# Summing three products of weights and values: one VectorE operation over a strided view in place of two additions

## The reference

```python
def attn(x, ...):                          # H = 16 heads, DH = 16
    xp = x @ Wp.T + bp
    q = ((xp @ Wq.T + bq) * scale).reshape(b, s, H, DH)
    k, v = ...                             # in the same way
    idx = stack([(i - 1) % s, i, (i + 1) % s], axis=1)
    kn, vn = k[:, idx], v[:, idx]
    attn = softmax(einsum('bshd,bsnhd->bshn', q, kn), axis=-1)
    out = einsum('bshn,bsnhd->bshd', attn, vn).reshape(b, s, d)
    return out @ Wo.T + bo

x = x + 0.5 * ffn(layernorm(x))
x = x + attn(layernorm(x))
x = x + 0.5 * ffn(layernorm(x))
```

## Time and profile before

| | us |
|---|---|
| median of 3 runs | 1087.7 (1087.16 to 1088.61) |
| the profiled execution's own time | 1087.54 |
| its span, first to last instruction | 1085.7 |
| TensorE busy | 1033.5 (95%) |
| VectorE busy | 861.3 (79%) |
| GpSimd busy | 716.6 (66%) |
| ScalarE busy | 544.9 (50%) |

### The profile page before, as it was taken

The page is one execution under the profiler, slowest core; times in us unless marked ns, Lnnn a source line. Parts: engine busy times, 40 slices in busy tenths (PEclk is TensorE's granted clock), DMA queues, the critical chain, the costliest instruction groups (busy, mean ns, idle before and its releaser), DMA issues.

```text
span 1085.7 us, 17486 instructions
## 1 busy us (share of the span) xinstructions
PE 1033.5 (95%) x5277; PEld 850.7 (78%) x5277; DVE 861.3 (79%) x2405; ACT 544.9 (50%) x1219; POOL 716.6 (66%) x956
## 2 busy tenths in 40 slices
PE   5889899999999999999999999999999999999785
PEld 3677788888888888888888888888888888887663
DVE  3648888888888888888888888888888888888882
ACT  4264455554545555554555555445555554544431
POOL 3366677666668777666777666677777766664453
PEclk9899999999999999999999999999999999999998
DMA  5001000000000000000000000000000000000000
GB/s 169 11 28 37 15 21 20 3 19 21 21 20 21 20 15 7 20 20 21 20 21 20 13 9 20 20 21 20 20 21 1 21 20 20 11 11 10 11 10 20
DMA packets 12613, 23.02 MB, mean 21 GB/s; under 512 B 2244, under 2 KB 5844, under 8 KB 12520
## 3 DMA queue, kind: packets, MB, share of 16 engines
q1 hardware_dynamic: 9240, 13.37, 3.5%
q0 software_dynamic: 3280, 8.53, 2.8%
HBM read 12.46 MB, written 8.39 MB: 19 GB/s over the span
## 4 chain that ended last, share of the span: by engine, by line
PE 87%; DVE 6%; issue 2%; DMA 1%; ACT 1%; SPq 0%; POOL 0%; DVEq 0%; POOLq 0%; ACTq 0%
PE ffn_bank L906 20%; PE ffn_bank L908 20%; PE ffn_bank L907 20%; PE tr_bank L935 5%; PE mix_bank L906 4%; PE mix_bank L908 4%; PE mix_bank L907 4%; PE tr_bank L948 3%; PE mix_bank L980 2%; PE tr_bank L906 1%; PE tr_bank L907 1%; PE tr_bank L908 1%; DMA we_raw<-in_L_ffn_We 1%; PE tr_bank L955 1%; DVE chain_sum L674 1%
## 5 line engine op out<-in xcount | busy, mean ns | idle before, releaser
L906 PE MATMUL ffn_bank<-we_hi,T_hi 128*128 128x512 f32 x1024 | 410.4, 401 | 3.8 <-DVE chain_sum L674 3.0
L908 PE MATMUL ffn_bank<-we_hi,T_lo 128*128 128x512 f32 x1024 | 401.3, 392 | 0.0
L907 PE MATMUL ffn_bank<-we_lo,T_hi 128*128 128x512 f32 x1024 | 400.8, 391 | 0.0
L465 ACT ACTIVATE we_raw<-ffn_bank,gate 128x256 f32<-128x256 f32 x512 | 207.4, 474 | 159.2 <-PE ffn_bank L908 159.0
L346 POOL TENSOR_TENSOR chain_sum<-chain_sum,we_raw 128x512 f32<-128x512 f32 x128 | 166.2, 1299 | 125.0 <-DVE chain_sum L674 124.7
L906 PEld LDWEIGHTS ffn_bank<-we_hi,T_hi 128*128 128x128 f32 x1024 | 193.0, 189 | 44.0 <-DVE chain_sum L674 4.6
L908 PEld LDWEIGHTS ffn_bank<-we_hi,T_lo 128*128 128x128 f32 x1024 | 193.0, 188 | 41.9
L907 PEld LDWEIGHTS ffn_bank<-we_lo,T_hi 128*128 128x128 f32 x1024 | 193.4, 189 | 35.2
L674 DVE SCALAR_TENSOR_TENSOR chain_sum<-ffn_bank,gate,chain_sum 128x256 f32<-128x256 f32 x256 | 111.4, 477 | 36.4 <-PE ffn_bank L908 36.4
L323 POOL TENSOR_TENSOR var_eps<-mean_var,eps 128x2 f32<-128x2 f32 x96 | 29.1, 303 | 151.3 <-DVE mean_var L594 151.3
L423 ACT CAST T_hi<-tr_bank 128x512 fp32r<-128x512 f32 x128 | 72.1, 590 | 106.6 <-PE tr_bank L935 86.3
(11 more groups left out here) (129 smaller groups left out, 1716.3 us busy)
## 6 DMA issues: line engine op xcount, KB each, us to landing
out_x<-y SPq DMA_DIRECT2D x31, 256.0 KB
we_raw<-in_L_ffn_We SPq DMA_DIRECT2D x2, 1024.0 KB, 13.9
x_in<-in_L_attn_x,x_row POOLq DMA_INDIRECT x60
x_in<-in_L_attn_x SPq DMA_DIRECT2D x2, 256.0 KB, 6.5
moved_qk<-qk SPq DMA_DIRECT2D x4, 124.0 KB
w_raw<-in_L_attn_Wq SPq DMA_DIRECT2D x1, 256.0 KB, 3.0
w_raw<-in_L_attn_Wk SPq DMA_DIRECT2D x1, 256.0 KB, 3.3
w_raw<-in_L_attn_Wv SPq DMA_DIRECT2D x1, 256.0 KB, 4.0
```

What stands on the lines that cost most here:

```text
L465: last = nc.scalar.activation(scaled[:, f, t, half, j], ffn_bank[b][:, j * D:(j + 1) * D], ACT.Copy, scale=gate[:, 2 * f + t, e:e + 1])
L906: nc.tensor.matmul(dest, hi[:, t, k, :], w_hi_[:, k, c0:c1], start=(first and k == 0), stop=False, skip_group_check=not first)
L907: nc.tensor.matmul(dest, hi[:, t, k, :], w_lo_[:, k, c0:c1], start=False, stop=False, skip_group_check=not first)
L908: last = nc.tensor.matmul(dest, lo[:, t, k, :], w_hi_[:, k, c0:c1], start=False, stop=(k == KB - 1), skip_group_check=not first)
```

## The change

The two additions become one `tensor_reduce` that adds along the innermost dimension of a rearranged view of `prod`: for each of the 512 output numbers the three inputs are 512 numbers (2 KiB) apart. It waits for count 14, where the first addition waited for 13, and raises the count by 2, so that a group still has 16 counts. The wait for `T_done[TO]` stands before it.

```diff
             def value_sum_step(a):
                 ops = attn_ops
-                dve.wait_ge(ops, a.times(ATTN_OPS, 13))
-                nc.vector.tensor_tensor(prod[:, 0], prod[:, 0], prod[:, 1], ALU.add).then_inc(ops, 1)
-                dve.wait_ge(ops, a.times(ATTN_OPS, 15))
+                dve.wait_ge(ops, a.times(ATTN_OPS, 14))
                 await_(dve, T_done[TO], a.times(1))
-                nc.vector.tensor_tensor(attn[:], prod[:, 0], prod[:, 2], ALU.add).then_inc(ops, 1)
+                nc.vector.tensor_reduce(attn[:].rearrange("p t n -> p (t n)"), prod[:].rearrange("p m t n -> p (t n) m"),
+                                        AX.X, ALU.add).then_inc(ops, 2)
```

## The result

The changed kernel takes 1090.9 us in the median of nine runs (1089.62 to 1092.96), against 1088.61 us for nine runs of the kernel before on the same footing (1086.52 to 1089.28). The ratio is 1.0026, with a 95% interval of 1.0017 to 1.0034: some 2.8 us slower, between 1.8 and 3.7 (the two medians are 2.3 us apart, the two means 3.0). The forecast was +1.6 us, to 1089.3 us, and "within 0.2%" as the likeliest; the time lies on the forecast side and in the range, a little beyond the 0.2%. Of the 1.6 us between 1089.3 and 1090.9, 0.9 are the base: the forecast stood on 1087.7 us, the median of three runs, and the nine runs of the kernel before have 1088.61.

A forecast was written before the change was run, and what follows sets the result against it. TensorE was taken to bound 130 to 967 us, so savings there count nothing; in the drain VectorE's sum lies on the path, 3 x 0.52 = +1.6 us on 1087.7, making 1089.3 us, range 1087.3 to 1093.5.

The forecast's parts named there:

- within 0.2%: Whole kernel: time differs from the kernel before by no more than about 0.2% (2.2 us); given 0.58.
- TensorE bounds the steady part: 29 groups outside the drain, fill included: some 15 us of saved VectorE time goes into idle time, gain nothing.
- The three groups of the drain carry the loss: Groups 29, 30 and 31: each ends its sum 0.52 us later, all passed on to TensorE, +1.6 us.
- The wait for the third product: Drain steps: waiting for count 14 rather than 13 makes the reduction begin 0.13 us later than line 747 did.
- The reduction's length: The new VectorE reduction of 1536 elements: taken as 1.80 us, ends 1.74 and 3.2 us.
- The first rival: Three drain steps: hops cost a turn each, reduction up to 3.2 us, +5.8 us, kernel 1093.5 us; chance 0.20.
- The second rival: Drain, behind TensorE's longer waits: granted clock falls once more, 1.7 us, kernel 1091.0 us; chance 0.15.

The follow-up runs named there:

- e1: Kernel before with the reduction in the 29 groups outside the drain, the two additions kept in groups 29, 30 and 31; ratio 0.9997.
- e6: Kernel before with the reduction done twice in each of the 29 groups outside the drain, additions kept in groups 29, 30 and 31; ratio 1.0017.
- e2: Kernel before with the reduction only in drain groups 29, 30 and 31, the two additions kept in the 29 others; ratio 1.0029.
- e4: The changed kernel run once more unaltered, as a yardstick on the same chip, against the kernel before; ratio 1.0028.
- e3: Kernel before with both additions kept, but the first waits for all three products (count 14 in place of 13); ratio 1.0004.
- after: The changed kernel, one reduction in place of the two additions in all 32 groups, against the kernel before; 1090.9 us, ratio 1.0026.
- e7: Kernel before, two additions kept, with the subtraction for pair 31 issued ahead of the value products in step 31; 1084.1 us, ratio 0.9962.
- e5: Kernel before plus eight reductions of 1536 numbers, in a row or stepped, behind VectorE's last instruction; only their durations read, 1741 to 2722 ns.
- e12: Kernel before plus eight reductions of 1536 numbers read in turn from 4 to 32 planes, behind VectorE's last instruction; durations 2.71 to 2.84 us.

## Why the prediction came out as it did

- *TensorE bounds the steady part, so the saving there is worth nothing.* Right: e1, 0.9997, and 838.3 us of steady part with either form. VectorE's 10 us and GpSimd's 20 us went into idle time. Wrong for the fill, which was counted in: by e6 a later sum in group 0 is passed on whole, and only the equal lengths there, 1.91 and 1.92 us, kept it out of the result.
- *The three groups of the drain carry the loss, and pass it on whole.* Right: e2 equals e4, and the offsets of the two traces grow by 0.67, 0.68 and 0.65 us at just these places.
- *The wait for the third product costs 0.13 us a step.* Right, 0.13 by e3's rows.
- *The reduction's length.* This is the term that was mis-sized. The prediction had 1.93 us from line 717's 12 ns, "if that grows with the elements", and took 1.80. It grows: 1.93 measured, 1.91 in the drain. With the 0.06 us of later start this makes 0.67 rather than 0.52 a step, 2.0 rather than 1.6 us in all. The probe without any neighbour shows the hops' part alone: 1.91 us against 1.75 in a row. The reason given for 1.80, that the hop cost almost nothing in line 717, was a reason about 96 numbers.
- *The first rival, a turn for each hop, 3.2 us.* Did not come; the probes show that a cost of this kind needs four planes. The Trainium skill's 1.73 ns a column (Vector Engine (DVE) Microarchitecture Reference, section 5.2) agrees with the probes from four planes on: 2.73 us less the fixed 143 ns of the earlier trace rows is 1.68 ns a number. For two planes the runs show 1.06, as that section's exception of two alternating regions has it; for three they show 1.15, and there the measurement decides against the 1.73. The 3.2 us themselves came from a misreading of line 747 beside GpSimd. It does not get every second turn, it waits for GpSimd's operation to end and then runs at its own rate. In the step of the earlier trace rows GpSimd's line 346 ends at 625.43 + 1.29 = 626.72 us and line 747 at 627.26, 0.54 later; line 348 ends at 627.86 and line 750 at 628.41, 0.55 later. In 26 steps from 157 to 939 us all 52 additions end 0.54 to 0.57 us after a GpSimd addition does.

```profile
625.43 1.29 POOL L346 TENSOR_TENSOR chain_sum<-chain_sum,we_raw 128x512 f32<-128x512 f32 x1 [0.65 <-DVE chain_sum L674]
```

- *The second rival, one more fall of the clock, chance 0.15, priced as a separate case.* This is the step that was wrong. It was not an alternative to the forecast but came on top of it, in all three profiles with one reduction in each drain step (after, e4, e2), at a cost of 0.1, 1.5 and 1.3 us. The sum with both is 2.0 us and, on the mean, something below 1 us: the 2.8 that were measured; the second term is a remainder, not measured by itself. The rival's price, 1091.0 us, lies next to the measured 1090.9, but it stood on a base 0.9 us too low, so that nearness is in part luck. The prediction had the two rows that ask the question, a wait of 1.89 us with a fall behind it and one of 1.63 without, and 1.63 + 0.5 lies above 1.89, as the prediction itself computed ("2.1 us") before it held against it that the waits come singly.
- *Within 0.2% the likeliest.* Hence missed by little: 0.26% (0.17 to 0.34), a case to which 0.38 was given.

## What to carry to other kernels

Before a cost per element is called fixed, multiply it by the size of the new operation and look at what both readings give; a pattern seen at 96 elements and a size seen at 1536 are two rows, and their product was the answer here. An engine's saved time is worth what the waiting engine gains at that place: 27 of 32 groups saved VectorE time under a full TensorE, in two there was nothing to save, and three met additions that were undisturbed and therefore shorter than the reduction, so the same edit should be made where two additions collide with GpSimd and left out where they don't (e1), which here gains nothing either. When a wait of TensorE grows, ask in the same sum whether its clock will fall behind it, and look for what else is queued behind the long operation: moving one subtraction ahead of it (e7) was worth more than the whole edit.

## What the runs showed of the hardware

- A VectorE reduction of 1536 float32 numbers from SBUF takes 1.74 to 1.75 us whether it makes 96, 512 or 768 outputs of numbers in a row; read in turn from 2 planes 1.77, from 3 planes 1.91 (1.88 at a step of 4), from 4 to 32 planes 2.71 to 2.84 (e5, e12). The steps ranged from 4 to 768 numbers.
- Two float32 additions of 512 numbers on VectorE take 0.68 us each alone and 1.1 to 1.5 us each beside GpSimd's additions, since the two engines take turns by whole operations (52 of 52 end 0.54 to 0.57 us after one of GpSimd's); the reduction takes 1.906 to 1.943 us beside the same, and GpSimd's additions of 256 numbers of line 348 fall from a mean of 0.81 to 0.74 us.
- TensorE's granted clock fell behind the 1.89 us wait of group 29 in the kernel before and not behind the 1.92 us at the same place in e6. In the changed kernel's first profile it fell behind waits of 2.59 and 2.36 us and not behind one of 2.28. A fall cost between 0.1 and 1.5 us, by whether TensorE had another wait just behind it.
